# One queue for the weight-conversion loads, two queues for the attention-weight loads

## What is computed

```python
xn = _layernorm(x, axis=-1)
x = x + attn(xn) + ffn(xn)

# attn: 16 heads of 64, causal, linear position bias, temperature
qkv = x @ W_attn + b_attn
att = einsum('bqhd,bkhd->bhqk', q, k) / sqrt(64) / temperature + bias
y = einsum('bhqk,bkhd->bqhd', softmax(att), v) @ W_proj + b_proj

# ffn: 3072 hidden, weights given as int32, scaled by 1/127
h = silu(x @ wg.T) * (x @ wu.T)
return h @ wd.T
```

## Time and profile before

| | us |
|---|---|
| median of 2 runs | 2136.66 (2134.55 to 2138.76) |
| the profiled execution | 2142.1 |
| its span (first to last instruction of the slowest core) | 2140.6 |
| spans of the eight cores | 2113.1 to 2140.6 |

### The profile page before, as it was taken

How to read it: one execution, slowest core, us unless ns; L and a number is a source line. 1 busy time by engine, 2 the same in 40 slices (tenths; PEclk the granted TensorE clock), 3 DMA queues, 4 the chain that set the end, 5 groups by cost and what they waited for, 6 DMA issues and landing times.

```text
span 2140.6 us, 26179 instructions; the slowest of 8 cores (2113.1 to 2140.6 us)
## 1 busy us (share of the span) xinstructions
PE 1347.7 (63%) x8642; PEld 699.9 (33%) x8642; DVE 946.6 (44%) x1601; ACT 921.9 (43%) x1745; POOL 77.5 (4%) x148
## 2 busy tenths in 40 slices
PE   0000018989899898359986665665646575657676
PEld 0000003434344343124433433433434343432333
DVE  2333330011011011144218686776868686854663
ACT  2333333203022031000138676777768676852442
POOL 0000000000000000013100000000000000000000
PEclk9998559999999999779995555555555555556778
DMA  6666444334244251442300101010010101022212
GB/s 207 235 233 227 168 147 160 126 98 158 99 135 141 68 168 63 152 164 77 106 28 13 60 1 60 1 45 16 4 57 1 60 1 60 1 73 76 79 60 89
DMA packets 46187, 198.86 MB, mean 93 GB/s; under 512 B 6119, under 2 KB 6120, under 8 KB 38378
## 3 DMA queue, kind: packets, MB, share of 16 engines
q1 hardware_dynamic: 29386, 130.09, 18.7%
q0 software_dynamic: 14080, 48.24, 6.2%
q10 hardware_dynamic: 2592, 18.88, 2.4%
HBM read 157.34 MB, written 39.85 MB: 92 GB/s over the span
## 4 chain that ended last, share of the span: by engine, by line
PE 49%; DMA 16%; DVE 12%; issue 11%; ACT 10%; DVEq 0%; SPq 0%; ACTq 0%; POOL 0%; POOLq 0%
PE ps_dn L405 8%; PE ps_g L361 8%; PE ps_u L369 8%; PE ps_tr L774 6%; DVE snegp L662 6%; PE ps_qk L491 5%; PE ps_tr L875 4%; ACT ptb L738 4%; ACT pbuf L698 4%; PE ps_y L799 3%; DMA abcp<-alibi_bc 3%; PE ps_v L527 3%; PE ps_s L643 2%; DVE ncmx L624 2%; DMA wst<-wattn 2%
## 5 line engine op out<-in xcount | busy, mean ns | idle before, releaser
L662 DVE SCALAR_TENSOR_TENSOR snegp<-ps_s,abcp 128x1024 f32<-128x1024 f32 (+2 forms) x320 | 330.5, 1058 | 247.7 <-PE ps_s L649 247.4
L738 ACT ACTIVATE ptb<-ps_tr 128x512 bf16<-128x512 f32 (+3 forms) x640 | 313.2, 531 | 278.1 <-PE ps_tr L774 273.6
L774 PE MATMUL ps_tr<-ident_s,pbuf 128*128 128x128 bf16 x2176 | 289.8, 295 | 186.6 <-ACT ptb L738 88.8
L624 DVE TENSOR_REDUCE ncmx<-snegp 128x2 f32<-128x1024 f32 (+2 forms) x320 | 328.4, 1052 | 3.5
L698 ACT ACTIVATE pbuf<-snegp,negmax 128x128 bf16<-128x128 f32 (+15 forms) x256 | 305.2, 1195 | 36.4 <-DVE negmax L679 34.8
L774 PEld LDWEIGHTS ps_tr<-ident_s,pbuf 128*128 128x128 bf16 x2176 | 191.1, 128 | 302.5 <-issue 292.1
L643 PE MATMUL ps_s<-k_hp,q_hp 64*128 64x512 bf16 (+2 forms) x320 | 143.0, 507 | 166.3 <-DVE snegp L662 93.7
L295 PE MATMUL ps<-ident_s,xn_st 128*128 128x128 bf16 x128 | 16.2, 305 | 304.6 <-DVE xn_st L278 304.6
L405 PE MATMUL ps_dn<-wdres,hbuf 128*128 128x512 bf16 x768 | 175.9, 389 | 37.9 <-DVE xfout L426 32.4
L361 PE MATMUL ps_g<-xnT,wgbuf 128*128 128x512 bf16 x768 | 183.1, 382 | 7.4 <-DMA wubuf<-wu_sc 7.4
L369 PE MATMUL ps_u<-xnT,wubuf 128*128 128x512 bf16 x768 | 181.5, 379 | 0.0
(11 more groups left out here) (65 smaller groups left out, 1049.7 us busy)
## 6 DMA issues: line engine op xcount, KB each, us to landing
wgbuf<-wg_sc SPq DMA_DIRECT2D x48, 512.0 KB
wubuf<-wu_sc SPq DMA_DIRECT2D x48, 512.0 KB
abcp<-alibi_bc SPq DMA_DIRECT2D x16, 1024.0 KB
wst<-wattn SPq DMA_DIRECT2D x8, 1536.0 KB
xstage<-xin SPq DMA_DIRECT2D x16, 512.0 KB
x2st<-xin POOLq DMA_DIRECT2D x16, 512.0 KB, 5.4
xf_sc<-xfout POOLq DMA_DIRECT2D x16, 512.0 KB, 3.0
xfst<-xf_sc SPq DMA_DIRECT2D x16, 512.0 KB
```

The costliest lines, as they stand in the source:

```text
L624: cd = S.op("vector", lambda e, par=par, c0=c0, w=w, ci=ci: e.tensor_reduce(ncmx[:, par * 8:par * 8 + 8].rearrange("p (j c) -> p j c", j=2 ...
L662: stt = S.op("vector", lambda e, par=par, hb=hp % 2, aoff=aoff, c0=c0, w=w, rA=rA: e.scalar_tensor_tensor(snegp[par].rearrange("p (j t) -> ...
L738: return e.activation(dst, src, AF.Copy)
L774: lasttr = S.op("tensor", lambda e, par=par, j=j, kc=kc, slot=slot, idx=idx, n=len(kcs): e.matmul(ps_tr[:, slot * 512 + (kc % 4) * 128: sl ...
```

## The change

Two queue names are changed. No instruction is added or removed.

```diff
@@ -193,7 +193,7 @@
                     src, dst_sc, j, width = conv_tasks[k]
                     bi = k % 3
                     b = k % 2
-                    lq = "sync" if k % 2 == 0 else "scalar"
+                    lq = "sync"
                     is_pj = (src == "wproj")
@@ -465,7 +465,8 @@
                 for dc in range(DC):
                     wb = dc % 2
-                    ld = S.dma("sync", lambda e, dc=dc, wb=wb: e.dma_start(
+                    ld = S.dma("sync" if wb == 0 else "scalar",
+                        lambda e, dc=dc, wb=wb: e.dma_start(
                         out=wst3[wb][:, :], in_=wattn[dc * 128:(dc + 1) * 128, :]),
                         waits=[("v", wst_war[wb])]
```

## The result

The changed kernel takes 2097.01 us (median of 13 runs) against 2139.64 us for the kernel before (median of 10), about 43 us less. The ratio is 0.9795, with a 95% interval of 0.9762 to 0.9827: faster beyond doubt, but whether by the full 2% the interval leaves open. In some executions the cores of one die run some per cent slower, whatever the kernel: the ratios in this text leave these out and the medians in us do not, and for the ring alone and for two queues early with the ring, whose profiled executions were of this kind, only stage 1 and the casts are read. The forecast was 46 us less, 2090.7 us, in a range of 2073 to 2120.

A forecast was written before the change was run, and what follows sets the result against it. Stage 1 was taken to be bound by a loop of waits with late odd loads. Gate and up -24, down weights -26, W_attn on two queues +4 gave -46 us, hence 2090.7 us from the median, range 2073 to 2120.

The forecast's parts named there:

- The bound: Stage 1: a loop of waits, odd loads issued late from ScalarE's list, DMA engines idle 28% and 51% between bursts.
- What is late next: Stage 1 after the change: the store; VectorE's store waits up from 43.9 us, load waits from 90.5 to under 30.
- Gate and up weights, -24: Stage 1, passes 0 to 7: passes of 18.9 us put task 23 at 160.3 instead of 184.35, -24 us.
- S: Landing time of a gate and up store in stage 1, taken as 8.1 us after the change, ends 6.1 and 10.1.
- turns of packets: Stage 1 stores: queues alternate by packet, so one load queue instead of two cuts the landing from 10.1 to 7.0 us.
- Down weights, -26: Stage 1, passes 8 to 11, no stores: 59.4 us to the first W_proj step instead of 85.9, -26 us.
- W_proj tasks, stage 2, 4 and 5: 0: W_proj tasks keep their buffer, queue and 51 us; stages 2, 4 and 5 hold no moved instruction and keep their lengths.
- B, +4: Stage 3, W_attn loads on two queues: paired loads land together, pairs take 11.7 us or more against 10.1, +4 us.
- Rival 1: Stage 1: the store binds, its landing stays at 10.1 us; -32 us in all, 2105 us; chance 0.23.
- rival 3: Stage 1: queues take turns of equal bytes, stores land in 5.4 us; -62 us in all, 2075 us; chance 0.17.
- Rival 2: Stage 1: one queue serves loads one after the other, latency included; +57 us in all, 2194 us; chance 0.03.
- Rival 4: Stage 1: moving the loads gains nothing, another wait takes its place at once; +4 us, 2141 us; chance 0.07.

The follow-up runs named there:

- the ring alone: Kernel before, with gate and up tasks scaled into a ring of four store slots, odd loads still late on the scalar queue; ratio to before 0.9998.
- two queues early with the ring: Kernel before, with odd loads issued early on the scalar queue and a ring of four store slots; ratio to before 0.969.
- B alone: Kernel before, with only pieces 1, 3, 5, 7 of W_attn moved to the scalar queue; ratio to before 1.0026.
- A alone: Kernel before, with only the int32 loads of stage 1 all on the sync queue, W_attn as before; 2094.16 us, ratio to before 0.981.
- two early queues: Kernel before, odd loads still on the scalar queue but each issued right behind ScalarE's step of task k-3; ratio to before 0.987.
- one queue with late loads: All stage 1 int32 loads on sync, odd loads also waiting for all ScalarE has been given so far; ratio to before 1.003.
- the change's A with odd loads behind step k-3: All stage 1 int32 loads on sync, odd load k also waiting for ScalarE's step of task k-3; ratio to before 0.983.
- A with the ring: All stage 1 int32 loads on sync, plus a ring of four store slots for gate and up tasks; ratio to before 0.9728.

## Why the prediction was right, point by point

**The bound.** The reading that stage 1 was bound by late odd loads between which the DMA engines rested is shown: the late wait put back on one queue takes the whole gain away, and early issue on two queues gives back all of it where there are no stores.

**What is late next.** The store, as named. Waits for stores were to rise above 43.9 us and are 77.6; waits for loads were to fall under 30 and are 16.8. Of the other signs, the DMA share was to be 0.85 to 0.9 over the first 230 us and is 0.80 from 11.2 on. Stage 2's first load was to be issued near 272 us and goes out at 277.8 on the slowest core (321.7 before), since stage 1 was shortened by 44 us and not 50.

**Gate and up weights, -24.** Measured -20.1 between the two profiled cores, -21.6 between the medians. The pass of 10.8 + S with S = 8.1 was to be 18.9 us; the medians give (160.0 - 24.6 - 3.3) / 7 = 18.9 us. The row of the store instructions, changed kernel, gives a median landing of 7.9 us:

```profile
DMA to landing us min/median/max: 4.1/7.9/12.1
```

So S was sized well, but the step that led to it failed. It said that the store would land sooner because it shares with one queue of loads instead of two, with 10.1 us as the value of before. That row was the longest of 24; the median before was 8.1:

```profile
DMA to landing us min/median/max: 4.0/8.1/10.1
```

The landing did not get shorter from before to after; on single cores the medians were 6.7 to 8.4 us before and are 7.3 to 8.1 after. Fewer queues and more loads beside each store cancelled, or neither mattered; the runs don't tell which. The fall from 10.1 to 7.0 by turns of packets did not take place, and the microsecond added to it "because loads will now lie beside every store" brought S to the value that it had all along. That S = 8.1 came out is luck. The forecast of -24 started from core 3, the last of the cores before (184.4, median 181.6); the medians go from 181.6 to 160.0, beside the forecast 160.3.

**Down weights, -26.** Measured -24.0 (medians 84.5 to 60.9: -23.6). VectorE still waits 10.2 us for these loads; the sum had allowed 1.5 and the 0.2 us a pass by which the bytes exceed the conversions. The stretch takes 61.9 us instead of 59.4.

**W_proj tasks, stage 2, 4 and 5: 0.** Measured +0.4 and -0.1, and 1207.7 us for the rest on both sides. Over the eight cores this rest is 1191 to 1209 us before and 1192 to 1209 after, with medians of 1205.8 and 1206.1, so the risk that the granted clock of the attention stage might shift did not come up.

**B, +4.** Measured +0.8 between the profiled cores, +0.5 and +1.3 in the medians. The step that failed is the size of the time between the loads of a pair: the sum took 1.8 us, the length of a cast, and so a period of 11.7. With B alone the casts of a pair stand 2.8 to 4.4 us apart, and with 3.6 the same sum gives 2.3 + 9.4 - 3.6 + 1.8 = 9.9 us; the casts come round every 9.8. The first cast was to be 4 us late. It is 1.1 us late with B alone (8.4 us after the start of stage 3, 7.3 before) and not at all in the changed kernel (7.2). A second step had no term: the issue on the scalar queue itself stood in the sum at nothing. In the changed kernel the first one takes 5.2 to 6.3 us, and the second cast stands 14.2 us after the start of stage 3, after 12.3 before and 11.4 with B alone. The rule of turns by packet from the Trainium skill, "DMA: Bandwidth & Descriptors", section "Queues, rings and completion order", fits the loads of a pair landing closer together here; it did not by itself give a price.

**Rivals.** Rival 1 (S stays at 10.1) and rival 3 (S falls to 5.4) are ruled out as numbers by the median landing of 7.9. In its mechanism rival 1 was nearer than the forecast, since the landing did stay; only its 10.1 was the longest store instead of the median. Rival 2, slower because one queue can't overlap its loads, is ruled out by 281 GB/s at a share of 0.88. Rival 4 is ruled out by A alone.

The Trainium skill, "DMA: Bandwidth & Descriptors", section "Issuing engines are not separate DMA queues", says that DMAs from all issuing engines run on the same 16 engines and that spreading them saves only issue time. The stretch without stores agrees (61.5 us with one queue, 59.0 with two early ones). In the stretch with stores two early queues are slower than one by 7.5 us, of which 3.3 are the start; whether the rest is a cost of the second queue, which the sentence doesn't have, is not shown.

## What to carry to other kernels

In this kernel a load that stands in ScalarE's list is issued when ScalarE gets there, not when its buffer is free; in such a case look in the timeline for the time between the two before counting queues. Where two waits alternate on one engine, taking one away may bring nothing, and the same edit may bring its full worth once the other is gone: the list of waits was not a price list here (44 us of waits for stores were worth 4 us at most up to stage 2 in the kernel before, and once edit A had raised them to over 70 us the same ring was worth 17). After a wait is removed, name what is late next and price it, since here the store loop kept 17 us that a ring of four slots gave back. And check the term you want against more than one row: the longest of 24 stores was taken for the usual one.

## What the runs showed of the hardware

How long a 0.5 MB store takes to land differs from kernel to kernel. Landing of the 24 gate and up stores, slowest core, in this order: one queue with late loads, the change's A with odd loads behind step k-3, two queues early with the ring:

```profile
DMA to landing us min/median/max: 2.9/3.9/11.4
...
DMA to landing us min/median/max: 4.4/8.7/11.3
...
DMA to landing us min/median/max: 7.0/11.5/17.2
```

The medians go from 3.9 to 11.5 us for the same bytes. The shortest belongs to the kernel with the emptiest DMA engines (a share of 0.65 from 28 us to task 23), the longest to one with full engines (0.96); but before and after the change it is 8.1 and 7.9 us at 0.72 and 0.88, so the share alone does not set it. And one queue with never more than two 1 MB loads outstanding, beside the stores, fills the DMA engines to a share of 0.96 at 308 GB/s in A with the ring: here two outstanding loads were enough when neither was late.
